# Attention kernel with paged keys: the output products of a group are spread over other steps, and its residual is added one step into the group that follows

## The reference

```
x = x + einsum('bct,bcd->bdt', x, weights[subjects])
q, k, v = x Wq, x Wk, x Wv;   q, k = rope(rmsnorm(q)), rope(rmsnorm(k))
k_all, v_all = concat(cache[block_table], new k / v)      # 512 + 32 keys
probs = softmax(mask(q k_all / sqrt(128)));   o = probs v_all
x = x + einsum('bse,de->bsd', o, Wo)                      # the output products
```

## Time and profile before

| | |
|---|---|
| median of 3 runs | 997.86 us (997.36 to 998.01) |
| profiled execution, its own time | 997.4 us |
| its span | 995.6 us |
| PE busy | 959.1 us, 96% |
| DVE busy | 828.0 us, 83% |
| ACT busy | 761.1 us, 76% |
| POOL busy | 579.0 us, 58% |

### The profile page before, as it was taken

How to read it: one execution, slowest core, us unless ns; L and a number is a source line. 1 busy time by engine, 2 the same in 40 slices (tenths; PEclk the granted TensorE clock), 3 DMA queues, 4 the chain that set the end, 5 groups by cost and what they waited for, 6 DMA issues and landing times.

```text
span 995.6 us, 25120 instructions
## 1 busy us (share of the span) xinstructions
PE 959.1 (96%) x8075; PEld 797.6 (80%) x8075; DVE 828.0 (83%) x1842; ACT 761.1 (76%) x2108; POOL 579.0 (58%) x861
## 2 busy tenths in 40 slices
PE   6899999999899999899999999999999999989998
PEld 4678888888677778788888888888888888878885
DVE  7789999999998689888878888888887887877880
ACT  5898999988884688888777778777877777777770
POOL 5565665655893057666755666565556555655550
PEclk9999999999999999999999999999999999999999
DMA  5899999989998989999999998999998999999950
GB/s 195 285 307 338 320 381 374 383 286 379 399 365 264 342 306 352 342 308 269 292 313 270 289 304 285 296 295 271 329 269 274 334 283 260 308 291 284 262 133 11
DMA packets 249907, 294.92 MB, mean 296 GB/s; under 512 B 79024, under 2 KB 206512, under 8 KB 247216
## 3 DMA queue, kind: packets, MB, share of 16 engines
q1 hardware_dynamic: 231088, 226.07, 76.4%
q0 software_dynamic: 18688, 67.25, 18.2%
HBM read 231.77 MB, written 46.27 MB: 279 GB/s over the span
## 4 chain that ended last, share of the span: by engine, by line
PE 75%; DVE 10%; POOL 6%; issue 5%; ACT 2%; DMA 2%; SPq 0%; DVEq 0%; ACTq 0%; POOLq 0%
PE ps_proj L1533 17%; PE ps_y L1533 16%; PE ps_o L1614 14%; PE ps_s L1571 8%; PE ps_t L1585 7%; PE ps_s L1575 7%; PE ps_rt L1709 2%; POOL vs L944 2%; DVE c_stage L1429 1%; POOL probs L963 1%; DVE rot L1405 1%; PE ps_o L1626 1%; DVE rot L1397 1%; DVE probs L1267 1%; DVE stage L1415 1%
## 5 line engine op out<-in xcount | busy, mean ns | idle before, releaser
L1039 ACT ACTIVATE probs<-probs,neg_max 128x544 f32<-128x544 f32 x256 | 191.6, 749 | 114.1 <-DVE neg_max L1267 97.3
L1267 DVE CUSTOM_DVE_ANT_0 probs<-ps_s,mask,row_scale 128x544 f32<-128x544 f32 x256 | 200.5, 783 | 52.3 <-PE ps_s L1575 41.2
L1614 PE MATMUL ps_o<-pt,vs 128*128 128x128 f16 x3072 | 213.3, 219 | 0.9 <-DMA vs<-v_pages,v_row 0.8
L1614 PEld LDWEIGHTS ps_o<-pt,vs 128*128 128x128 f16 x3072 | 192.4, 98 | 15.8 <-DMA vs<-v_pages,v_row 1.6
L963 POOL TENSOR_SCALAR probs<-probs,recip 128x512 f32<-128x512 f32 x144 | 99.8, 693 | 167.8 <-DVE recip L1275 164.2
L909 POOL TENSOR_TENSOR roped<-rot 128x256 f32<-128x256 f32 x160 | 144.1, 922 | 79.9 <-DVE rot L1397 75.9
L1533 PE MATMUL ps_proj<-wt_hi,x0t_hi 128*128 128x512 f32 x384 | 159.1, 415 | 6.2 <-DVE x0t_lo L1223 5.8
L1287 DVE SCALAR_TENSOR_TENSOR pt<-ps_t,pt 128x512 f16<-128x512 f32 x190 | 130.4, 686 | 36.7 <-ACT pt L1045 30.9
L1533 PE MATMUL ps_y<-wo,ot_hi 128*128 128x512 f16 x512 | 153.3, 381 | 0.0
L1533 PE MATMUL ps_proj<-wt_hi,x0t_lo 128*128 128x512 f32 x384 | 150.7, 394 | 0.0
L1533 PE MATMUL ps_proj<-wt_lo,x0t_hi 128*128 128x512 f32 x384 | 149.8, 391 | 0.0
(11 more groups left out here) (162 smaller groups left out, 1811.8 us busy)
## 6 DMA issues: line engine op xcount, KB each, us to landing
kt<-k_pages_t SPq DMA_DIRECT2D x512, 128.0 KB
c_nat<-in_L_cond_k_cache SPq DMA_DIRECT2D x32, 512.0 KB, 6.0
q_t<-stage SPq DMA_DIRECT2D x64, 256.0 KB, 6.3
c_nat<-in_L_cond_v_cache SPq DMA_DIRECT2D x32, 512.0 KB, 7.2
qt<-q_t SPq DMA_DIRECT2D x32, 512.0 KB
w_nat<-in_L_cond_Wq SPq DMA_DIRECT2D x8, 1024.0 KB, 7.5
k_pages_t<-c_stage SPq DMA_DIRECT2D x16, 512.0 KB, 5.2
c_nat<-in_L_cond_Wo SPq DMA_DIRECT2D x16, 512.0 KB, 6.5
```

What stands on the lines that cost most here:

```text
L1039: act.activation(pr, pr, ACT.Exp, bias=col(neg_max, i), scale=-1.0, accum_out=col(row_sum, i)).then_inc(a_exp, 1)
L1267: dve.tensor_tensor_reduce(out=probs_of(i), in0=ps_s[:, score_cols(i):score_cols(i) + KEYS], in1=mask[(i // HK) % 2][:, mask_at(i):mask_at ...
L1614: ins = pe.matmul(ps_o[n % 2][:, jl * P:(jl + 1) * P], v[:, part, :], pt[pt_slot(i)][:, NCH * half + c, :], start=jl == 1 and c == 0 and k ...
```

## The change

In groups 0 to 6 the heads stand at other steps. Before, steps r = 0, 30 and 31 have no output products; now r = 0, 17 and 29 have none. Head 19 and those after it move by one step (r = 18 to 28), and heads 30 and 31 move from r = 28 and 29 to r = 30 and 31. The residual of a group, which DVE adds at the beginning of r = 30, is now added at the end of r = 0 of the group that follows. For the last group neither the products nor the residual move; only the residual of group 6, which its first product waits for, moves from step 254 to step 256.

```diff
-    Y_AT = {1: (0, 1), 2: (2,), 3: (3,), 4: (4, 5), 5: (6, 7)} | {r: (r + 2,) for r in range(6, HQ - 2)}
+    Y_AT = ({1: (0, 1), 2: (2,), 3: (3,), 4: (4, 5), 5: (6, 7)} | {r: (r + 2,) for r in range(6, 17)}
+            | {r: (r + 1,) for r in range(18, HQ - 3)} | {r: (r,) for r in (HQ - 2, HQ - 1)})
...
     def y_out(i):
 
-        g = y_group(i)
-        return g if g >= 0 and i - GSTEPS * (g + 1) == (Y_OUT if g + 1 < NG else Y_OUT_LAST) else None
+        if i == GSTEPS * NG + Y_OUT_LAST:
+            return NG - 1
+        g, r = divmod(i, GSTEPS)
+        return g - 2 if r == 0 and g >= 2 else None
...
             for i in range(STEPS):
-                if y_out(i) is not None:
+                if i >= NP2 and y_out(i) == NG - 1:
                     add_residual(y_out(i))
...
                 if by_dma(i + 2):
                     rows_lo(i + 2)
+                if y_out(i) is not None and y_out(i) + 1 < NG:
+                    add_residual(y_out(i))
```

More of the change, by code:

```diff
@@ L511, in held_by @@
         return max((m for m in range(n) if t_banks[m] == t_banks[n]), default=-1)
-    Y_AT = {1: (0, 1), 2: (2,), 3: (3,), 4: (4, 5), 5: (6, 7)} | {r: (r + 2,) for r in range(6, HQ - 2)}
+    Y_AT = ({1: (0, 1), 2: (2,), 3: (3,), 4: (4, 5), 5: (6, 7)} | {r: (r + 2,) for r in range(6, 17)}
+            | {r: (r + 1,) for r in range(18, HQ - 3)} | {r: (r,) for r in (HQ - 2, HQ - 1)})
     Y_LAST = {1: range(0, 8), 2: range(8, 16), 3: range(16, HQ)}
-    Y_OUT, Y_OUT_LAST = HQ - 2, 4
+    Y_OUT_LAST = 4
     ONE_TURN = 16
```

## The result

The changed kernel takes 1009.53 us (median of 5 runs, 1007.35 to 1011.59), 1.0112 times the time of before, 95% interval [1.0099, 1.0125]. It is slower, as forecast, but by more: 1003.5 was forecast, and the range ended at 1006.5. In later runs beside the kernel before it had 1007.82 against 997.38 us, ratio 1.0104 [1.0085, 1.0123]. The profiled execution took 1011.59 us, its span 1009.8.

What follows compares the result with a forecast made beforehand. In phase 2 PE's own work and its losses at group ends were taken as the bound. Terms 3.3 + 0.1 + 2.3 gave +5.7 us, own time 997.4 to 1003.1, median 1003.5 us, range 1000 to 1006.5.

Steps and rivals of the forecast that it cites:

- the 0 us for the emptied steps: At r = 17 and 29, PE running 0.65 us ahead was taken to cost 0 us.
- the last end: At i = 256, the later residual delays the last group's head 0, all of it counting: +2.3 us.
- The chain: At a group's end, head 31, `ot_hi_of`, `exp`, `tn_hi`, `tn_lo`, residual in sequence; head 0 starts at about 658.45; 68 in 100.
- no new wait: Rival at group ends: the old loss goes, head 0 finds its bank free; 993.4 us, 7 in 100.
- a shorter chain: Rival: chain 0.6 us shorter at each end, five ends free, last end 1.7 us; 999.6 us, 11 in 100.
- the Trainium skill's rule on rotating PSUM banks: Between head 31 and head 0, pricing the evacuation alone exposes nothing; sum -4.5 us.
- An end costs 0.66 us more than before: At five ends, i = 96 to 224, head 0 starts 0.66 us later than before; 3.3 us together.
- the old loss: At ends after three steps without heads, PE loses 0.75 us; six ends would give back 4.5 us.
- waits at r = 17 to 31: Sign in the changed trace: PE waits at these steps would show the prediction wrong.
- The one forecast row on slack: At r = 29, the second half of the scores starts 0.42 us after the maximum frees its bank.
- this rival: Steps 17 and 29 cost too, up to 0.65 us each, 9.1 us at most; half gives 1008; 12 in 100.
- The clock rival: Clock falls to half after the last end's wait, costing the 32 heads up to 21 us; 2 in 100.

Runs made afterwards that it cites:

- the trace at full clock: Profiled fastest execution of e14, at full clock throughout; its stretches sum to +8.40 us over the kernel before.
- e1: Changed kernel with the residual ahead of `tn_lo` at r = 0; 998.59 us, 1.0004 times the kernel before.
- e2: Kernel before's table of heads, with only the residual moved to the end of r = 0; 1007.51 us, 1.0096 times the kernel before.
- e13: e11 with step r = 26 empty in place of r = 17 in groups 0 to 5; 996.91 us, 0.9988 times the kernel before.
- e14: Changed kernel with step r = 26 empty in place of r = 17; 1006.41 us, 1.0103 times the kernel before.
- e3: Changed kernel, but group 6 keeps the old table and its residual stays at step 254; 1003.15 us, 1.0052 times the kernel before.
- e4: Changed kernel with nine unused 512-column matmuls ahead of the last group's head 0; 1006.83 us, 1.0087 times the kernel before.
- e5: Changed kernel with `exp` ahead of `ot_hi_of` at r = 31 on ACT; 1012.36 us, 1.0158 times the kernel before.
- e9: Changed kernel with the unused matmuls of both e4 and e6; 1005.63 us, 1.0077 times the kernel before.
- e11: Changed kernel with e1 and e3 together; 997.71 us, 0.9998 times the kernel before.
- e12: e11 with two more unused gathers ahead of phase 2; 1000.46 us, 1.0025 times the kernel before.
- e6: Changed kernel with nine unused 512-column matmuls ahead of the transposes of step 222; 1005.96 us, 1.0085 times the kernel before.
- e8: Kernel before, unchanged, run once more; 998.35 us, 1.0008 times the kernel before.
- e10: Kernel before with two more unused gathers ahead of phase 2; 998.88 us, 1.0017 times the kernel before.
- e15: Kernel before with nine unused 512-column matmuls ahead of the transposes of step 222; 997.26 us, 0.9996 times the kernel before.
- e16: e13 with nine unused 512-column matmuls ahead of the transposes of step 222; 994.63 us, 0.9972 times the kernel before.
- the fill: Nine unused 512-column matmuls ahead of the transposes of step 222, added in e6, e9, e15 and e16; in e6 1005.96 us.
- e7: Changed kernel, unchanged, run once more; 1007.82 us, 1.0104 times the kernel before.

## Why the prediction was right in its direction and too small

The sum was +5.7 us, and the trace at full clock has +8.4. Of the 2.7 us between them 0.9 lie at i = 64, 0.4 at the four ends from i = 96 to 192, 0.5 at i = 224 and 0.8 at the last end. The steps that failed are the 0 us for the emptied steps, and the terms for the last end and for i = 224, which were made too small. The clock and the waits for gathered values come on top in single executions.

**The chain: right.** Each link forecast is in the trace, and head 0 came 0.06 us from where it was put. e1 shows that the residual's place behind `tn_lo` makes the wait, since one step in DVE's order takes it away at six of seven ends. e2 shows that the chain need not begin at head 31: with the old table, where head 31 is long done, head 0 waits 0.99 us as well. The rivals of no new wait and of a shorter chain fall. Of the Trainium skill's rule on rotating PSUM banks, which read by the bare evacuation gave -4.5 us, e1 shows what the sum turns on: at six of seven ends the evacuation does fit between head 31 and head 0 when `tn_lo` does not stand ahead of it. I called the wait about 1.4 us. The trace has 1.01 at the product and the 0.29 at the scores of r = 1, where DVE's queue makes itself felt first.

**"An end costs 0.66 us more than before": mis-sized, 0.77 in the clean trace.** 0.06 of it is the chain, and 0.05 more PE's start behind the wait: head 0 to head 1 takes 661.60 - 660.90 = 0.70 instead of 0.65. Over four ends that is 0.4.

**"I take 0 us for these two steps" (17 and 29): failed in group 1, and at r = 18 in some executions.** This is the step of the prediction that I had read from one group alone. The prediction named waits at r = 17 to 31 as a sign that it is wrong, and one of 0.43 us stands at r = 18. In group 1 ACT and DVE still scale pieces of `wo`, and they are the bound there, not PE. PE in group 1, r = 17 to 19, before (first fence) and changed (second):

```profile
462.37 0.60 PE L1533 MATMUL ps_y<-wo,ot_hi 128*128 128x512 f16 x2
...
463.46 0.57 PE L1571 MATMUL ps_s<-kt,qt 128*128 128x320 f16 x3
...
467.07 0.49 PE L1571 MATMUL ps_s<-kt,qt 128*128 128x256 f16 x3
```

```profile
463.23 0.66 PE L1590 MATMUL ps_t<-fixed,probs 128*128 128x128 f32 x4 [0.16 <-POOL probs L960]
463.73 0.57 PE L1576 MATMUL ps_s<-kt,qt 128*128 128x320 f16 x3
...
467.60 0.49 PE L1576 MATMUL ps_s<-kt,qt 128*128 128x256 f16 x3
```

ACT at the same place, before and changed:

```profile
464.33 0.71 ACT L1082 ACTIVATE wo<-wo,scale 128x512 f16<-128x512 f32 x1
...
466.88 0.57 ACT L1045 ACTIVATE pt<-ps_t 128x512 f16<-128x512 f32 x1
```

```profile
464.86 0.71 ACT L1085 ACTIVATE wo<-wo,scale 128x512 f16<-128x512 f32 x1
...
467.42 0.58 ACT L1048 ACTIVATE pt<-ps_t 128x512 f16<-128x512 f32 x1
```

The changed trace is 0.53 us late on all engines here, from phase 1. The head of the emptied step (462.37) is gone, yet at 467.60 PE is again 0.53 behind and not 0.12 ahead. It waited the head's 0.65 away, for POOL and ACT, and does the head later on top. That is 0.65 of the +1.08 at i = 64. With r = 26 empty instead (e13, e14) PE waits there too, 0.52 us at r = 27, and i = 64 costs the same. The other 0.4 is the exchange of the old loss for the wait at head 0 (0.52), where I had 0.1. The one forecast row on slack, 0.42 us in group 3, said nothing about group 1.

The waits for gathered values at r = 18 are the same step in the other groups. They differ between executions: 0.43 us in one trace of the changed kernel and 0.3 in the other, 0.79 in e1, 0.62 in e3 (and 1.30 at r = 26), 0.3 in e4, 0.9 in e5, 0.5 in e9, 1.2 in e11, 1.0 in e12, and none in e6. None of the traces with the old table (before, e8, e10, e15, e2) or with step 26 empty (e13, e14, e16) has one; in those PE isn't ahead at r = 18. I named late weights of POOL as this rival's danger, and the 0.42 us of the maximum; in the middle groups neither came. It was the transfer.

**The last end, forecast 2.3, is 3.1: mis-sized, 0.8 of the 2.7 us missed at full clock.** The wait for the residual is 2.40 at 982.55. Another 0.51 is a wait I did not have, at 974.75: with no scores to do from step 253 on and two heads fewer done than before, PE comes to the transposes of step 254 and asks for the bank of `ps_t` before `tn_lo` has read it. The forecast held that "the weighing of r = 0 starts at 653.87 with or without the change, if PE waits nowhere before", and moved that assumption to the last group, where a step has less work on PE. 0.17 is spread over the rest.

**i = 224: 1.2 and not 0.66.** The long wait of step 223, 2.4 us in the earlier trace rows, stands behind POOL's gather of step 220. That gather takes 1.46 us in the changed kernel and 1.03 in the kernel before. PE's wait grows from 2.42 to 2.84. The wait of POOL ahead of the gather is 2.84 to 2.85 in all the traces, so it isn't the change's. With the fill the changed kernel has 1.03 as well. What sets the 1.03 or the 1.46 is open.

**The clock rival: its reasoning fell, its chance of 2% was too small.** I argued that a wait of 2.4 us had left the clock at 1.00, so that waits no longer than this would too. In the traces of these kernels the same place did both:

| wait of PE, us | granted clock fell to half behind it | stayed full |
|---|---|---|
| 2.93, step 223 | | e2 |
| 2.84, step 223 | changed, e7, e1, e3, e4, e12 | e5, e11, e13, e14 |
| 2.42, step 223 | e10 | before, e8 |
| 2.40, last end | changed, e6 | e7, e14, e5 |
| 1.90, last end | e2 | |
| 0.89 and 0.86, i = 192 | e5, once of six ends | |

What was wrong is to take one execution for a threshold. A fall costs 1.7 us for each 3.4 us of work at half clock, not the up to 21 I had put beside it. The Trainium skill (TensorE: Matmul & The Clock Gate, Part 1) says that the gate's own timing runs free and doesn't start with the kernel, so that one program sees the change at different places from run to run. The table agrees: behind the same wait of 2.40 us the changed kernel fell in its first trace and not in e7. In the medians of the later series the clock weighs nothing, since both kernels have a mean of 0.9972 there. In the first series the changed kernel has 0.9956, which by the same mean is 0.0016 of 1010 us or 1.6 us more (an estimate); the means don't say where in the program the falls lie.

**What is left.** The table's sum at full clock, 8.4 us, is a ratio of 1.0085. The two ratios measured are 1.0112 [1.0099, 1.0125] and 1.0104 [1.0085, 1.0123]. The second reaches down to it, the first does not. About 1.6 us of the first is the clock. The waits at r = 18 could make up some of the other 2 us. So could chance in phase 1, which the change doesn't touch: from the start to the first cut of the table the traces take 450.8 to 455.5 us. No run here separates them.

## What to carry to other kernels

When a result bank has one owner, the price of emptying it is the whole in-order queue ahead of the instruction that empties it, not that instruction. Put it ahead of whatever it doesn't need: here one step in DVE's order took away 1.2 us an end. A slot that PE gives up is worth something only where PE is the bound, and this has to be read in every group, the first and the last above all: one had other work on ACT and DVE, and the other had less on PE.

A term that the change makes at the same place seven times should be read at all seven places before it is multiplied.

## What the runs showed of the hardware

- TensorE's granted clock fell to half behind waits of 0.9 to 2.84 us in some executions and stayed full behind the same waits in others; a fall lasted 3.4 us, or 6.8 once in phase 2 (changed kernel at 894.6).
- Nine unused matmuls just ahead of the long wait cost nothing measurable in the kernel before (0.9996 [0.9983, 1.0009]). With them GpSimd's gather of step 220 takes 1.03 us in the variants of the changed kernel (3 traces), and without them 1.45 to 1.53 (11 traces).
- GpSimd waits 2.84 us ahead of the gather of step 220, in the kernel before and in every variant, and two gathers more ahead of it did not move it to another step. Its cause is not known.
